# Normalised tile 3 transposed by DMA instead of by TensorE, in a gated cross-attention and mixture block on one core

## The chip, the cores and the metric

The kernel runs on one core of a Trainium2 chip. The metric is the device time of one execution, in microseconds. PE stands for TensorE (PEld for its weight loads), DVE for VectorE, ACT for ScalarE, POOL for GpSimd and SP for SyncE, which here only issues DMAs.

## The reference

The input x has 2 batches of 512 rows of 1024 floats, the context 2 batches of 1024 x 1024. What is computed, with fake_quant(v, s, z) = (clip(round(v / s + z), 0, 255) - z) * s:

```python
x = x + tanh(g_xattn) * matmul(fake_quant(layernorm(x), s1, z1), fake_quant(ctx, s2, z2))
n = layernorm(x)
gate = softmax(n @ W_gate.T)                                  # 8 experts
thr = sigmoid(n @ W_thr + b_thr) * 0.125
w = maximum(gate - thr, 0); w = w / sum(w)                    # sum 0 counts as 1
base = n @ W_base.T + b_base
moe = einsum('ner,ne,eor->no', (n @ A_w.T), w, B_w) * 2       # rank 16
x = x + tanh(g_ffn) * (base + moe)
```

## The kernel before

**Tiles.** The 1024 rows are 8 tiles t = 0 to 7 of 128 rows, tiles 0 to 3 of batch 0 and 4 to 7 of batch 1. Every engine has a hand-written order of instructions; the engines meet through semaphores, and the same names stand in each engine's list.

**Stage A, per batch, the quantised product.** `affine_q1` (ACT) and `round_q1` (DVE) turn the normalised rows into bf16 integers q1; `affine_ctx` (ACT) and `round_ctx` (DVE) do it for 8 chunks of the context. q1 of batch 0 is transposed by PE, q1 of tiles 4 to 7 by DMA (`transpose_q1` on SP, L299). `first_half` and `second_half` (L913) are the products of batch 1, `add_product` (DVE, L708) adds them to x in `xs`, POOL sums the context columns (`sum_k`, L408 and L413) for `column_sums` (L979), and adds the result (`add_columns`).

**Stage B, per tile t, the mixture.** `normalise(t)` (ACT, L511) writes the second layernorm's rows to `work`. They are needed transposed and split into a high part `lnTh` and a low part `lnTl` of type fp32r. `combined(t, i)` (PE, L1035 to L1037) multiplies them with the weights, also split, in three pieces i = 0, 1, 2 of the output columns: 24 matmuls for a piece. Piece 0 holds the gate's columns. After it come, on DVE and ACT, the steps of the gate: `gate_max` (DVE L732), `gate_exps` (ACT L542, L543), `gate_weights` (DVE L739 to L751, ends in `hw`). PE transposes `hw` in `flip_hw(t)` (L1050), ACT and DVE split that (L502, L722), and `moe` (L1059 to L1061) adds the experts' part. `add_row_term` (ACT L484), `add_bias` (POOL L430) and `finish` (DVE L763) close the tile, SP stores it.

**Two ways to transpose the normalised tile.** For tiles 0 to 4 PE does it: `flip_ln(t)` (L1023), 8 fp32 transposes of 128x128 into two PSUM banks, between `combined(t - 1, 0)` and `combined(t - 1, 1)`. ACT (`split_hi`) and DVE (`split_lo`) read the banks. The two banks 6 and 7 are used by turns by `flip_ln` and `flip_hw`, so that `flip_hw(2)` waits until DVE has read the first half of tile 3. For tiles 5 to 7 (`by_dma`) it goes by DMA: `halve(t)` (ACT L520) copies the tile as two blocks of 16-bit halves into ring slot 3, `transpose_ln(t)` (SP L292) transposes them into ring slot 4, `join(t)` (ACT L529) interleaves them to floats in ring slot 5, `joined_hi(t)` (ACT L535) and `joined_lo(t)` (DVE L726) split them.

**Order round the change.** PE does the mixture of tiles 0, 1, 2, then, at t == `A1_AFTER` = 3, both halves of batch 1's product, then the mixture of tiles 3 to 7. ACT in pass t = 1, after `split_hi(hw, 1)`: `normalise(3)`, `affine_q1(6)`, `affine_q1(7)`, `affine_ctx(11)`, `affine_ctx(12)`; in pass t = 2: `gate_exps(2)`, `add_row_term(2)`, the two `split_hi` of tile 3, `affine_ctx(13)`, `split_hi(hw, 2)`. DVE in pass t = 2: `gate_max(2)`, `gate_weights(2)`, the two `split_lo` of tile 3, `split_lo(hw, 2)`, `round_q1(7)`, `round_ctx(13)`, `finish(2)`, `round_ctx(14)`. SP: the store of tile 0, `transpose_q1` of tiles 4, 5 and 6, the store of tile 1, `transpose_q1(7)`.

**Memory.** `ring` has 6 slots of 4 KB a partition. Slots 3, 4 and 5 hold at that time the context chunks 10, 11 and 12. `colbc` (4 KB a partition) holds the regrouped weights of B until PE has transposed them in pass t = 0, and from `scale_columns(1, 0)` on the column terms of batch 1.

Of the kernel before, what the change touches and what calls it, by code (L numbers as in the profile page):

```python
# [21 lines left out]
U16 = mybir.dt.uint16  # L22
# [5 lines left out]
P = 128  # L28
# [6 lines left out]
def gated_block(nc, x, ctx_in, g_x, g_f, x1_scale, x1_zp, x2_scale, x2_zp,  # L35
                W_base, b_base, W_gate, W_thr, b_thr, A_w, B_w, out):
    B, S, D = x.shape
# [4 lines left out]
    MT = S // P  # L42
    T = B * MT
# [24 lines left out]
    turn_of = {key: n // NS + 1 for n, key in enumerate(chunks)}  # L68


    by_dma = [t for t in range(T) if t > MT]


    early = [("A", 0, 0), ("A", 0, 1), ("gates", 0, 0)] + [("W", o, i) for o in range(2) for i in range(NH)]
# [13 lines left out]
    flip_no = {key: n for n, key in enumerate(flips)}  # L88
# [32 lines left out]
    with es:  # L121
# [8 lines left out]
        ring = sb("ring", [P, NS, 2 * H])  # L130
# [38 lines left out]
        own_home["W", OWN_W + 3] = landing[:, after_WTl + 2 * O + 3 * D:after_WTl + 2 * O + 4 * D]  # L169

        halves = ring[:, 3, :].bitcast(U16)
        halvesT = ring[:, 4, :].bitcast(U16).rearrange("p (b t) -> p b t", t=P)
        lnT = ring[:, 5, :]

        def home(key):
            return own_home[key] if key in own_home else ring[:, slot_of[key], :]
# [81 lines left out]
        @block.sync  # L258
        def _(sp):
            def load_x(t):  # L260
                b, m = t // MT, t % MT
                sp.dma_start(xs[:, t, :], x[b, m * P:(m + 1) * P, :]).then_inc(x_loaded[t], 16)

            def load_own(key):
                dst, src = source(key)
                sp.dma_start(dst, src).then_inc(own_loaded[key], 16)

            def load(n):
                key = chunks[n]
                if n >= NS:  # L270
                    old = chunks[n - NS]
                    if old[0] == "ctx":
                        sp.wait_ge(ctx_affine, old[1] + 1)
                    elif old[0] == "B":
                        sp.wait_ge(b_regrouped, 1)
                    else:
                        last = (old[0], old[1], 0 if old[0] == "gates" else 1)
                        sp.wait_ge(flipped, flip_no[last] + 1)
                s = slot_of[key]
                if key[0] == "gates":  # L280
                    sp.dma_start(ring[0:E, s, :], W_gate).then_inc(slot_loaded[s], 16)
                    sp.dma_start(ring[E:E + 1, s, :], W_thr.rearrange("(a d) -> a d", a=1)).then_inc(gates_loaded, 16)
                else:
                    dst, src = source(key)
                    sp.dma_start(dst, src).then_inc(slot_loaded[s], 16)

            def transpose_ln(t):
                n = by_dma.index(t)
                sp.wait_ge(ln_halved, n + 1)
                if n:  # L290
                    sp.wait_ge(ln_joined, n)
                sp.dma_start(halvesT, halves, transpose=True).then_inc(ln_transposed[t], 16)  # L292

            def transpose_q1(t):
                m = t % MT
                sp.wait_ge(q1_ready, t + 1)
                if m == 0:
                    sp.wait_ge(prod_ready, NH * MT)
                sp.dma_start(q1T[:, :, m * P:(m + 1) * P], q1[:, t % 2, :], transpose=True).then_inc(q1_transposed[m], 16)  # L299

            for t in range(MT):
                load_x(t)
            for c in range(CPB):
                load_own(("ctx", c))
            for n in range(NS):
                load(n)
            for o in range(OWN_W, O // P):
                load_own(("W", o))
            load_x(MT)
            load_x(MT + 1)  # L310
            load(NS)
            sp.dma_start(tb[:, :], b_base.rearrange("(a d) -> a d", a=1).to_broadcast([P, O])).then_inc(s_bias, 16)
            load_x(MT + 2)
            load_x(MT + 3)
            for n in range(NS + 1, len(chunks)):
                load(n)
            for t in range(T):
                b, m = t // MT, t % MT
                if t < T - 1:
                    sp.wait_ge(out_part, NP * (t + 1))  # L320
                    sp.dma_start(out[b, m * P:(m + 1) * P, :], xs[:, t, :]).then_inc(s_stored, 16)
                    if t + 3 == A1_AFTER:
                        transpose_q1(MT)
                        transpose_q1(MT + 1)
                        transpose_q1(MT + 2)
                    if t + 2 == A1_AFTER:
                        transpose_q1(MT + 3)
                    if t + 3 in by_dma:
                        transpose_ln(t + 3)
                else:  # L330
                    for i, (_, c, n) in enumerate(outp):
                        sp.wait_ge(out_part, NP * t + i + 1)
                        sp.dma_start(out[b, m * P:(m + 1) * P, c:c + n], xs[:, t, c:c + n]).then_inc(s_stored, 16)
            sp.wait_ge(s_stored, 16 * (T - 1 + NP))
# [124 lines left out]
        def _(act):  # L459
# [12 lines left out]
            def affine_ctx(c):  # L472
                arrived(act, ("ctx", c))
                s = home(("ctx", c))
                if c >= NU:
                    act.wait_ge(q2_ready, c - NU + 1)
                nc.scalar.activation(q2u[:, c % NU, :], s, ACT.Identity, bias=Z2, scale=R2).then_inc(ctx_affine, 1)  # L477
# [36 lines left out]
            def halve(t):  # L514

                n = by_dma.index(t)
                if n:
                    act.wait_ge(ln_transposed[by_dma[n - 1]], 16)
                act.wait_ge(ln_ready, t + 1)
                nc.scalar.copy(halves.rearrange("p (h c) -> p h c", h=2),  # L520
                               work[:, t % NW, :].bitcast(U16).rearrange("p (c h) -> p h c", h=2)).then_inc(ln_halved, 1)

            def join(t):

                n = by_dma.index(t)
                if n:
                    act.wait_ge(ln_lo, n)
                act.wait_ge(ln_transposed[t], 16)
                nc.scalar.copy(lnT.bitcast(U16).rearrange("p (c h) -> p h c", h=2),  # L529
                               halvesT.rearrange("p (h k) t -> p h (k t)", h=2)).then_inc(ln_joined, 1)  # L530

            def joined_hi(t):
                act.wait_ge(ln_joined, by_dma.index(t) + 1)
                act.wait_ge(base_part, NP * (t - 1))
                nc.scalar.copy(lnTh[:, t % 2, :], lnT).then_inc(ln_hi, 1)  # L535
# [39 lines left out]
            for t in range(T):  # L575
                if t + 1 == MT:
                    normalise(MT)
                if t == 0:

                    arrived(act, ("B", 0))  # L580
                    act.wait_ge(cols_added, NH * MT - len(own_col_adds))
                    act.wait_ge(x1_part, NH * MT)
                    nc.scalar.activation(colbc[:, :].rearrange("p (j e r) -> p e j r", j=8, e=E),
                                         ring[:, slot_of["B", 0], :].rearrange("p (e j r) -> p e j r", e=E, j=8),
                                         ACT.Identity, scale=SCALING).then_inc(b_regrouped, 1)
                gate_exps(t)
                add_row_term(t)
                if t == 0:
                    for key in late[10:12]:
                        split_hi(key)  # L590
                if t + 1 in by_dma:
                    join(t + 1)
                elif t + 1 < T:
                    split_hi(("ln", t + 1, 0))
                    split_hi(("ln", t + 1, 1))
                if t + 1 == A1_AFTER:
                    affine_ctx(CPB + 5)
                split_hi(("hw", t, 0))
                if t + 1 in by_dma:
                    joined_hi(t + 1)  # L600
                if t == 0:
                    for key in late[12:]:
                        split_hi(key)
                if t + 2 < T and t + 2 != MT:
                    normalise(t + 2)
                if t + 2 in by_dma:
                    halve(t + 2)
                if t + 3 == A1_AFTER:
                    affine_ctx(CPB)
                    affine_ctx(CPB + 1)  # L610
                    affine_ctx(CPB + 2)
                    affine_q1(MT)
                    affine_q1(MT + 1)
                if t + 2 == A1_AFTER:
                    affine_q1(MT + 2)
                    affine_q1(MT + 3)
                    affine_ctx(CPB + 3)
                    affine_ctx(CPB + 4)
                if t + 1 == A1_AFTER:
                    affine_ctx(CPB + 6)  # L620
                    affine_ctx(CPB + 7)
                    scale_columns(1, 0)
                    scale_columns(1, 1)
# [546 lines left out]
```

## Time and profile before

| what | value |
|---|---|
| three runs | 185.35, 187.31 and 186.85 us, median 186.85 us |
| the profiled execution, its own time | 185.18 us |
| its span, first to last instruction | 183.4 us (1.8 us lie around it) |
| PE busy | 173.0 us |
| DVE, ACT, POOL busy | 112.8, 90.6, 71.9 us |

A busy share is a mean over stages with different limits. All times of rows are microseconds from the start of the span unless marked ns; a name like L1035 is a line of the kernel. The ends of matmuls are modelled: in a run of them their starts tell the pace.

### The profile page before, as it was taken

The numbers are of one execution on the slowest core, as the hardware profiler recorded it, in microseconds if no ns is written. First come the engines' busy times: TensorE is split into PE (matmuls) and PEld (weight loads), VectorE is DVE, ScalarE is ACT, GpSimd is POOL, SyncE is SP. The second block draws the span as 40 slices with busy tenths as digits, with TensorE's granted clock in tenths as the row PEclk, the third lists the DMA queues.
The fourth block names the chain that finished last, engine by engine and source line by source line (L and its number), as shares of the span: only waits on it lengthen the run. The fifth ranks groups of instructions, "written<-read, shape, count | busy, mean of one in ns | idle before, by whom it ended". The sixth has DMA issues, their size and how long they took to land.

```text
span 183.4 us, 2896 instructions
## 1 busy us (share of the span) xinstructions
PE 173.0 (94%) x1058; PEld 150.5 (82%) x1058; DVE 112.8 (62%) x281; ACT 90.6 (49%) x123; POOL 71.9 (39%) x89
## 2 busy tenths in 40 slices
PE   4869999989999998999899999999999999999993
PEld 4755446568899998999864479999999999999992
DVE  1999895989588988978852673583351351351331
ACT  2399914665987938194810106160970970820300
POOL 3560024921001395299868787045500500500400
PEclk9999999999999999999999999999999999999999
DMA  6999999999030332065040000006209008002003
GB/s 223 307 390 386 390 410 405 363 395 380 33 116 0 119 110 118 0 118 172 12 135 29 0 0 0 4 0 114 114 0 228 4 0 229 2 4 114 2 0 114
DMA packets 19934, 25.39 MB, mean 138 GB/s; under 512 B 11207, under 2 KB 12615, under 8 KB 19920
## 3 DMA queue, kind: packets, MB, share of 16 engines
q1 hardware_dynamic: 19906, 25.21, 40.6%
q8 instruction: 8, 0.13, 0.3%
q14 instruction: 6, 0.05, 0.1%
q10 hardware_dynamic: 14, 0.00, 0.0%
HBM read 18.39 MB, written 4.19 MB: 123 GB/s over the span
## 4 chain that ended last, share of the span: by engine, by line
PE 67%; DVE 17%; ACT 5%; DMA 4%; issue 3%; POOL 2%; DVEq 0%; ACTq 0%; POOLq 0%
PE bank L913 14%; PE bank L1035 13%; PE bank L1037 13%; PE bank L1036 13%; DVE st L654 5%; DVE q L689 2%; PE bank L995 2%; DMA q1T<-q 2%; PE bank L971 2%; DMA xs<-in_x_dram 2%; PE bank L1061 2%; PE bank L1060 2%; PE bank L1059 2%; DVE WTl L722 1%; ACT WTh L502 1%
## 5 line engine op out<-in xcount | busy, mean ns | idle before, releaser
L1035 PE MATMUL bank<-WTh,lnTh 128*128 128x388 f32 (+1 forms) x192 | 67.2, 350 | 0.0
L1037 PE MATMUL bank<-WTh,lnTl 128*128 128x388 f32 (+1 forms) x192 | 65.1, 339 | 0.0
L1036 PE MATMUL bank<-WTl,lnTh 128*128 128x388 f32 (+1 forms) x192 | 65.0, 338 | 0.0
L1035 PEld LDWEIGHTS bank<-WTh,lnTh 128*128 128x128 f32 x192 | 36.2, 189 | 0.3
L1036 PEld LDWEIGHTS bank<-WTl,lnTh 128*128 128x128 f32 x192 | 36.2, 189 | 0.0
L1037 PEld LDWEIGHTS bank<-WTh,lnTl 128*128 128x128 f32 x192 | 36.1, 188 | 0.0
L430 POOL TENSOR_TENSOR xs<-xs,tb 128x1024 f32<-128x1024 f32 x8 | 19.3, 2408 | 39.8 <-ACT xs L484 39.8
L913 PE MATMUL bank<-q,q1T 128*128 128x512 bf16 x128 | 30.3, 379 | 0.2 <-DVE q L689 0.2
L424 POOL TENSOR_TENSOR xs<-xs,colbc 128x512 f32<-128x512 f32 x14 | 18.0, 1313 | 15.9 <-DVE xs L708 11.1
L913 PEld LDWEIGHTS bank<-q,q1T 128*128 128x128 bf16 x128 | 12.1, 98 | 14.3 <-DVE q L689 0.6
L654 DVE BATCH_NORM_STATS2 st<-xs 128x6 f32<-128x512 f32 x32 | 20.7, 681 | 4.2 <-DMA xs<-in_x_dram 4.2
L763 DVE SCALAR_TENSOR_TENSOR xs<-bank,con,xs 128x250 f32<-128x250 f32 (+2 forms) x24 | 13.1, 571 | 15.4 <-PE bank L1061 11.8
L542 ACT ACTIVATE gt<-bank,con 128x1 f32<-128x1 f32 x8 | 2.1, 260 | 31.6 <-DVE gt L732 31.6
L413 POOL TENSOR_TENSOR colacc<-colacc,q 128x512 f16<-128x512 f16 x12 | 15.1, 1256 | 3.3 <-DVE q L689 2.2
L511 ACT ACTIVATE work<-xs,cf 128x1024 f32<-128x1024 f32 x8 | 10.0, 1247 | 11.0 <-POOL cf L398 11.0
L708 DVE SCALAR_TENSOR_TENSOR xs<-bank,con,xs 128x512 f32<-128x512 f32 x16 | 11.3, 745 | 6.5 <-PE bank L913 6.4
L397 POOL TENSOR_TENSOR cf<-cf,mhalf 128x1 f32<-128x1 f32 x8 | 4.4, 547 | 27.9 <-DVE cf L667 27.9
L469 ACT ACTIVATE q1u<-xs,cf 128x1024 uint8<-128x1024 f32 x8 | 9.8, 1239 | 6.6 <-DVE q L679 4.0
L502 ACT CAST WTh<-bank 128x512 fp32r<-128x512 f32 (+1 forms) x19 | 10.1, 573 | 5.8 <-PE bank L995 5.8
L689 DVE TENSOR_SCALAR q<-q2u 128x1024 bf16<-128x1024 uint8 x16 | 12.1, 777 | 0.5 <-ACT q2u L477 0.4
L722 DVE TENSOR_TENSOR WTl<-bank,WTh 128x512 fp32r<-128x512 f32 (+1 forms) x19 | 11.7, 658 | 1.1 <-ACT WTh L502 1.1
L491 ACT ACTIVATE colbc<-bank,con 128x512 f32<-128x512 f32 x4 | 2.7, 687 | 15.1 <-PE bank L979 9.5
(102 smaller groups left out, 230.7 us busy)
## 6 DMA issues: line engine op xcount, KB each, us to landing
xs<-in_x_dram SPq DMA_DIRECT2D x8, 512.0 KB, 7.3
landing<-in_ctx_dram SPq DMA_DIRECT2D x8, 512.0 KB, 10.8
ring<-in_ctx_dram SPq DMA_DIRECT2D x8, 512.0 KB, 6.8
out_dram<-xs SPq DMA_DIRECT2D x7, 512.0 KB, 2.9
ring<-in_L_ffn_W_base_dram SPq DMA_DIRECT2D x4, 512.0 KB, 13.2
landing<-in_L_ffn_W_base_dram SPq DMA_DIRECT2D x4, 512.0 KB, 15.9
ring<-in_L_ffn_A_w_dram SPq DMA_DIRECT2D x1, 512.0 KB, 12.8
ring<-in_L_ffn_B_w_dram SPq DMA_DIRECT2D x1, 512.0 KB, 6.5
```

What stands on the lines that cost most here:

```text
L413: nc.gpsimd.tensor_tensor(colacc[:, h, :], colacc[:, h, :], tile, ALU.add).then_inc(col_added, 1)
L424: nc.gpsimd.tensor_tensor(part, part, colbc[:, h * H:(h + 1) * H], ALU.add).then_inc(cols_added, 1)
L430: nc.gpsimd.tensor_tensor(xs[:, t, :], xs[:, t, :], tb[:, :], ALU.add).then_inc(xb_ready, 1)
L502: nc.scalar.copy(hi, src).then_inc(flip_hi, 1)
L654: nc.vector.bn_stats(st[:, t, h, :], xs[:, t, h * H:(h + 1) * H]).then_inc(dve_step, 1)
L689: nc.vector.tensor_scalar(q, q2u[:, c % NU, :].rearrange("p (k n) -> p k n", k=2), -CENTRE, None, ALU.add).then_inc(q2_ready, 1)
L722: nc.vector.tensor_tensor(lo, src, hi.bitcast(F32), ALU.subtract).then_inc(flip_read, 1)
L763: nc.vector.scalar_tensor_tensor(out=part, in0=bank[3 * j + i][:, a:a + n], scalar=TGF, in1=part, op0=ALU.mult, op1=ALU.add).then_inc(out_ ...
L913: return mm(bank[prod_bank(h, m)][:, :], q1T[:, k, m * P:(m + 1) * P], q2[:, k, h * H:(h + 1) * H], start=(k == 0), stop=(k == KT - 1))
L1035: mm(o, hi, WTh[:, k, a:b], start=(k == 0), stop=False, skip_group_check=True)
L1036: mm(o, hi, WTl[:, k, a:b], start=False, stop=False, skip_group_check=True)
L1037: ins = mm(o, lo, WTh[:, k, a:b], start=False, stop=(k == KT - 1), skip_group_check=True)
```

## The change

Tile 3 joins the tiles that are transposed by DMA. PE's `flip_ln(3)`, ACT's two `split_hi` and DVE's two `split_lo` of tile 3 are gone. ACT does `halve(3)` after `normalise(3)`, `join(3)` at the end of pass t = 1 and `joined_hi(3)` in pass t = 2 after `add_row_term(2)`; DVE does `joined_lo(3)` after `split_lo(hw, 2)`. SP issues `transpose_ln(3)` between `transpose_q1(5)` and `transpose_q1(6)`. Since chunks 11 and 12 still hold slots 4 and 5 then, tile 3's transposed halves go to `colbc`, and the joined tile of every `by_dma` tile now goes to slot 3, over the halves. So `halve` of a later tile waits for `joined_lo` of the tile before it, where it waited for its transpose.

```diff
-    by_dma = [t for t in range(T) if t > MT]
+    by_dma = [MT - 1] + [t for t in range(T) if t > MT]
...
-        halvesT = ring[:, 4, :].bitcast(U16).rearrange("p (b t) -> p b t", t=P)
-        lnT = ring[:, 5, :]
+        lnT = ring[:, 3, :]
+
+        def halvesT(t):
+
+            return (colbc[:, :] if t < MT else ring[:, 4, :]).bitcast(U16).rearrange("p (b t) -> p b t", t=P)
...
                 if n:
                     sp.wait_ge(ln_joined, n)
-                sp.dma_start(halvesT, halves, transpose=True).then_inc(ln_transposed[t], 16)
+                else:
+                    sp.wait_ge(flipped, flip_no["B", 0, 1] + 1)
+                sp.dma_start(halvesT(t), halves, transpose=True).then_inc(ln_transposed[t], 16)
...
                         transpose_q1(MT + 1)
+                        transpose_ln(MT - 1)
                         transpose_q1(MT + 2)
                     if t + 2 == A1_AFTER:
                         transpose_q1(MT + 3)
-                    if t + 3 in by_dma:
+                    if t + 3 in by_dma and t + 3 > MT:
                         transpose_ln(t + 3)
...
                 if n:
-                    act.wait_ge(ln_transposed[by_dma[n - 1]], 16)
+                    act.wait_ge(ln_lo, n)
                 act.wait_ge(ln_ready, t + 1)
...
             def join(t):
 
-                n = by_dma.index(t)
-                if n:
-                    act.wait_ge(ln_lo, n)
                 act.wait_ge(ln_transposed[t], 16)
...
-                if t + 1 in by_dma:
+                if t + 1 in by_dma and t + 1 > MT:
                     join(t + 1)
+                elif t + 1 in by_dma:
+                    joined_hi(t + 1)
                 elif t + 1 < T:
                     split_hi(("ln", t + 1, 0))
                     split_hi(("ln", t + 1, 1))
                 if t + 1 == A1_AFTER:
                     affine_ctx(CPB + 5)
                 split_hi(("hw", t, 0))
-                if t + 1 in by_dma:
+                if t + 1 in by_dma and t + 1 > MT:
                     joined_hi(t + 1)
...
                     affine_ctx(CPB + 3)
                     affine_ctx(CPB + 4)
+                    join(MT - 1)
```

## Rows read from the trace of the kernel before

**Rows 1.** The page: busy time by engine, and TensorE's granted clock in 40 slices.
```profile
PE 173.0 (94%) x1058; PEld 150.5 (82%) x1058; DVE 112.8 (62%) x281; ACT 90.6 (49%) x123; POOL 71.9 (39%) x89
...
PEclk9999999999999999999999999999999999999999
```

**Rows 2.** Timelines of PE and PEld: start us, us, instruction, idle before, releaser.
```profile
86.77 0.34 PE L1037 MATMUL bank<-WTh,lnTl 128*128 128x388 f32 x1
87.83 0.30 PE L1050 MATMUL bank<-idf,hw 128*128 128x128 f32 x1 [0.72 <-DVE lnTl L722]
...
93.63 1.90 PE L913 MATMUL bank<-q,q1T 128*128 128x512 bf16 x8
...
100.72 0.10 PEld L979 LDWEIGHTS bank<-colacc,ones_h 128*128 128x128 f16 x1 [0.29 <-issue]
```

**Rows 3.** Chain that ended last: start us, us, what.
```profile
77.49 3.67 DMA q1T<-q
...
87.01 0.68 DVE lnTl L722
...
88.13 0.18 PE bank L1035
...
112.30 0.87 PE bank L1023 x8
```

**Rows 4.** Timeline of ACT, passes t = 1 and t = 2.
```profile
72.26 1.25 ACT L511 ACTIVATE work<-xs,cf 128x1024 f32<-128x1024 f32 x1
77.50 2.38 ACT L469 ACTIVATE q1u<-xs,cf 128x1024 uint8<-128x1024 f32 x2 [3.99 <-DVE q L679]
79.79 2.36 ACT L477 ACTIVATE q2u<-ring,prm,con 128x1024 uint8<-128x1024 f32 x2
84.94 0.26 ACT L542 ACTIVATE gt<-bank,con 128x1 f32<-128x1 f32 x1 [2.79 <-DVE gt L732]
```

**Rows 5.** Timeline of DVE, pass t = 2.
```profile
86.66 0.35 DVE L751 SCALAR_TENSOR_TENSOR hw<-bank,gt 128x128 f32<-128x128 f32 x1
...
88.98 1.21 DVE L679 TENSOR_SCALAR_CACHE_REDUCE q<-q1u 128x1024 bf16<-128x1024 uint8 x1
```

**Rows 6.** Timeline of SP's queue: issue us, us, instruction.
```profile
77.49 2.69 SPq L299 DMA_TRANSPOSE q1T<-q  x2
...
82.52 1.23 SPq L299 DMA_TRANSPOSE q1T<-q  x1
...
90.22 1.24 SPq L299 DMA_TRANSPOSE q1T<-q  x1
```

**Rows 7.** q1 transposes (L299): from issue to landing, four of them.
```profile
DMA to landing us min/median/max: 3.0/3.1/3.7
```

**Rows 8.** Transposes of halves (L292), tiles 5 to 7: issue duration, landing.
```profile
L292 SPq DMA_TRANSPOSE ring<-ring x3: 1774/1849/1992, 124.0 to 150.5; - x3
...
DMA to landing us min/median/max: 4.2/4.3/6.0
```

**Rows 9.** Lines of tiles 5 to 7: duration ns min/median/max, first and last start.
```profile
L520 ACT COPY ring<-work x3: 1900/1900/1902, 122.1 to 148.5; 128x2048 uint16<-128x2048 uint16 x3
...
L529 ACT COPY ring<-ring x3: 2547/2547/2547, 129.6 to 157.7; 128x2048 uint16<-128x2048 uint16 x3
...
L535 ACT CAST lnTh<-ring x3: 1050/1051/1051, 132.2 to 160.5; 128x1024 fp32r<-128x1024 f32 x3
...
L726 DVE TENSOR_TENSOR lnTl<-ring,lnTh x3: 1224/1226/1226, 133.3 to 161.6; 128x1024 fp32r<-128x1024 f32 x3
```

**Rows 10.** ACT behind a join, pass t = 4.
```profile
129.64 2.55 ACT L529 COPY ring<-ring 128x2048 uint16<-128x2048 uint16 x1
132.03 0.28 ACT L502 CAST hwTh<-bank 128x128 fp32r<-128x128 f32 x1
```

**Rows 11.** Timeline of POOL: column additions that end before TensorE's 100.72.
```profile
91.13 2.41 POOL L413 TENSOR_TENSOR colacc<-colacc,q 128x512 f16<-128x512 f16 x2 [0.63 <-DVE q L689]
95.13 5.48 POOL L413 TENSOR_TENSOR colacc<-colacc,q 128x512 f16<-128x512 f16 x4 [1.59 <-DVE q L689]
```

More of the change, by code:

```diff
@@ L523, in join @@
             def join(t):
-                n = by_dma.index(t)
-                if n:
-                    act.wait_ge(ln_lo, n)
                 act.wait_ge(ln_transposed[t], 16)
                 nc.scalar.copy(lnT.bitcast(U16).rearrange("p (c h) -> p h c", h=2),
-                               halvesT.rearrange("p (h k) t -> p h (k t)", h=2)).then_inc(ln_joined, 1)
+                               halvesT(t).rearrange("p (h k) t -> p h (k t)", h=2)).then_inc(ln_joined, 1)
             def joined_hi(t):
```

## The prediction

> **What bounds the kernel now.** I read the page first [rows 1]: PE is busy 173.0 of 183.4 us, the next engine 112.8, and the granted clock is full (1.00, its 2.4 GHz level) in every slice. So time is saved where PE has less to do or waits less, and lost where it is made to wait. The reader should then ask at which places PE waits. Around the change there is one, in PE's timeline [rows 2]: the last matmul of `combined(2, 1)` starts at 86.77, and at the pitch of 0.18 of such matmuls [rows 3] PE would be free at 86.95; `flip_hw(2)` starts at 87.83. 0.88 us are lost. From there PE runs through `combined(2, 2)` and `moe` to the first product of batch 1 at 93.63 [rows 2], 5.80 us without a wait, and from then on to the end nothing but PE's own work is of weight in the chain.
>
> What does `flip_hw(2)` wait for? The row names DVE's `lnTl`, and the chain says the same: DVE reads the first half of tile 3 from the bank for 0.68 us from 87.01, and 0.14 later PE starts [rows 2, 3]. But `hw` itself is only ready at 86.66 + 0.35 = 87.01 [rows 5]. Two conditions lie 0.68 us apart. Further back stands `gate_exps(2)` on ACT at 84.94, which had waited 2.79 us for DVE's `gate_max` [rows 4]; DVE was late with it since it was rounding q1 and ctx, behind a q1 transpose of 3.67 us [rows 3]. From `gate_exps(2)` to `hw` ready is 87.01 - 84.94 = 2.07 us, a chain of small steps with no room.
>
> **What is taken away.** PE loses the 8 transposes of tile 3. In the chain the same 8 of tile 4 stand for 0.87 us [rows 3]. By that PE comes to `flip_hw(2)` at 86.95 - 0.87 = 86.08. It can't start there: `hw` is ready at 87.01. The bank wait goes too, as no tile 3 halves pass through the banks. So if nothing else moved, `flip_hw(2)` would start at 87.01 + 0.14 = 87.15, against 87.83: 0.68 us gained. The 0.87 of the transposes is hidden behind the gate and is not added. ACT's two splits and DVE's two are replaced by one of 1.05 on ACT and one of 1.23 on DVE [rows 9], about equal work.
>
> **What is added on ACT, and where it lands.** `halve(3)` takes 1.90 us [rows 9]. It follows `normalise(3)`, from 72.26 to 73.5, and ACT's next work starts at 77.50 after an idle 3.99 us [rows 4]: hidden, with 2 us to spare, cost nothing. `join(3)` takes 2.55 us [rows 9] and is queued between `affine_ctx(12)`, which ends at 79.79 + 2.36 = 82.15, and `gate_exps(2)`, now at 84.94 [rows 4]. The gap is 2.79 us, just long enough, if the join could start at 82.15 to 82.4. The question is whether tile 3's transpose has landed by then.
>
> It hasn't. SP issues q1's transposes of tiles 4 and 5 from 77.49 for 2.69 us, to 80.18, since they wait for DVE's `round_q1` [rows 6], and `transpose_ln(3)` stands behind them in SP's queue. Its own conditions (halves ready at 75.4, `colbc` free) are long met, so it is issued at 80.2. The three transposes of the same kind took 4.2, 4.3 and 6.0 us from issue to landing [rows 8]. Bounds: 84.4 with the shortest, 86.2 with the longest. Neighbours in the queue matter: of q1's four transposes [rows 7], the shortest had 3.0 and one 3.7, and the 3.7 is the one with another transpose right behind it [rows 3, 6]. Tile 3 has q1's tile 6 behind it, issued at 82.52 [rows 6]; SP is free for that by 80.2 + 1.8 = 82.0 [rows 8], so q1 itself isn't late. I take 4.3 plus 0.4, somewhat over half of q1's 0.7, landed at 84.9.
>
> The join then runs from 84.9; behind a join of 2.55 us the next instruction started 2.4 us after the join's start in one pass [rows 10], so I take 2.5 between that and the full length. `gate_exps(2)` starts at 87.45 in place of 84.94: 2.5 later. `hw` is ready 2.07 later, at 89.52, and `flip_hw(2)` starts at 89.66. Against 87.83 that is **+1.83 us**. Queued behind ACT's wait stand `gate_exps(2)`, `add_row_term(2)` and all of pass t = 2; PE, DVE and POOL wait for them. PE, free at 86.08, stands still for 3.6 us.
>
> The Trainium skill speaks against this change: "VectorE: DVE Perf Modes", Rules for kernel authors, says to transpose 128x128 on TensorE if a PSUM destination is fine, and by DMA otherwise. By it the sum would be a loss, and the working above agrees. A tile of halves is 512 KB, twice one of q1, and its shortest landing is 1.2 us longer, 4.2 against 3.0 [rows 7, 8]: 2.4 us for the 512 KB. "Advanced Engine Details and Errata", X-Bar Transpose, in the Trainium skill, expects 350 to 400 GB/s, by which they would take, as an estimate, 1.4 us; the landing would be 1.0 earlier and the loss 1.1 in place of 2.1. The rows decide.
>
> **The second place, tile 7 of q1.** In pass t = 2 all of ACT's list moves by 2.5. DVE's `round_q1(7)` was at 88.98 [rows 5] and stood behind `split_lo(hw, 2)`; now `joined_lo(3)`, 1.23 us [rows 9], stands between them, where the two splits it replaces stood before both and filled a wait of DVE. So `round_q1(7)` starts at 88.98 + 2.5 + 1.2 = 92.7, the transpose of tile 7 is issued at 90.22 + 3.7 = 93.9 [rows 6] and has landed at 96.9 to 97.0 [rows 7]. PE's product starts at 89.66 + 5.80 = 95.46 and comes to tile 7 after six of the eight matmuls that the row has in 1.90 us [rows 2], 1.3 us: 96.8. Before, it had landed at 93.2 and was wanted at 94.9, 1.7 us of cover; now the cover is gone and PE waits about 0.3 with the semaphore's delay. Bounds 0 and 0.7, the last if the landing takes 3.7. POOL meets it at the same point: its column additions of chunk 13 wait for `round_ctx(13)` and move 3.7, from 91.13 to 94.85, end at 97.3, and push those of chunks 14 and 15 (5.48 us from 95.13, end 100.61, PE's `column_sums(1)` at 100.72) by 2.1 in all [rows 2, 11]. That is the same 1.83 + 0.3, side by side, counted once.
>
> **Later tiles.** `halve(6)` and `halve(7)` now wait for `joined_lo` of the tile before. That takes 1.23 on DVE after `joined_hi`, while ACT does `normalise` in about 1.25 [rows 4, 9]: 0.1 later on ACT at most, and the transpose's wait is off PE's path. Nothing, for both.
>
> **The sum.** 1.83 + 0.3 = +2.1 us. Against the profiled execution, 185.18 (183.4 of span and 1.8 around it), that is 187.3. The median of the runs is 186.85, 1.67 above that execution; the same difference on it gives **188.9**, which I forecast, 1.1% slower. Within the mechanism: the join at 84.4, followed 2.4 later, and tile 7 in time gives +1.1; at 85.1 with the full 2.55 and 0.7 for tile 7 gives +2.8.
>
> **Rivals.**
> - *The join fits the gap* (other side: faster). If the transpose landed by 82.4, `gate_exps(2)` would stay at 84.94 and 0.68 us would be gained: 186.2. The point from which it decides is a landing at 84.9 - 1.83 = 83.1, 2.9 us after the issue. For it: ACT's gap is 2.79 us. Against: the shortest of three needs 4.2 [rows 8]. Chance 0.07.
> - *About even.* The landing comes a little sooner than any row (a faster transfer, as above), or the steps of the gate are quicker when DVE has nothing else to do: -0.4 to +1.1, 186.5 to 187.9. Chance 0.14.
> - *A slow transpose.* One of three took 6.0 [rows 8]. Landed at 86.2, everything is 1.3 later: +3.4, 190.3. Chance 0.12 for the median of several runs.
> - *The clock falls.* PE stands still for 3.6 us, while in the rows the clock is full throughout and there is no standstill of PE that long behind the start. At the lower level the 0.18 of a matmul becomes 0.36; the 5.80 us up to the product would take up to 11.6, of which I take a third, +1.9: +4, 190.9. Chance 0.05. The Trainium skill, "TensorE: Matmul & The Clock Gate", Part 1, states that an idle TensorE is set back to half clock; no row here shows it.
> - The forecast, +1.1 to +2.8 (187.9 to 189.7), has the other 0.62.
>
> **How the numbers follow.** About 1% (1.87 us) is what a measurement of this kernel can tell from no change; three runs spread over 1.96. Of the forecast's 0.62 some 0.34 lies above that bound, with 0.17 of the slow rivals 0.51: slower. Same: 0.28 of the forecast, 0.14, and most of the first rival, 0.46. Faster 0.03. The range leaves out the clock's case and the faster half of the first: 186.1 to 190.4.
>
> **What the profile will show.** ACT: L520 with about 1.9 us near 73.5, in idle time; L529 for tile 3 starting at 84.4 to 85.1, its releaser a DMA to `colbc`, and L542 right behind it near 87.4, no longer waiting for DVE. PE: 8 fewer L1023; L1050 of tile 2 after an idle of over 3 us, released by DVE's `hw`, not `lnTl`. SP: a third transpose at 80.2. PE idle of some tenths before the eighth product of batch 1. It would be wrong if the landing were under 3 us after the issue, or if PE had later waits that take the delay in; I found none.

## The result, and the profile after

The changed kernel takes 190.19 us (median of 6 runs, 189.26 to 190.38), the kernel before 186.66 (6 runs, 185.35 to 187.95). The ratio is 1.0186, 95% interval 1.0147 to 1.0225: 3.5 us slower. The profiled execution took 189.26 us with a span of 187.5, against 185.18 and 183.4. Beside the experiments the kernel before was measured again, 17 to 29 runs, medians 186.35 to 186.40; one execution of e3_ln_first that took 957.16 us is left out of its ratio.

Near the start the executions differ for reasons that have nothing to do with the change: in 8 of the 14 traces the clock falls once there, in the fourth slice of the page, and in others the work is late without that (`flip_hw(1)` starts at 72.70 in e1_late_join and at 73.18 in e9_warm_late_lo). So traces are compared below by their distance from `flip_hw(1)`, which starts at 71.73 before and at 71.94 after. 0.2 us of every difference between the two traces is that.

The page of the changed kernel, its busy times and its granted clock:

```profile
PE 173.2 (92%) x1044; PEld 151.2 (81%) x1050; DVE 113.3 (60%) x280; ACT 94.9 (51%) x124; POOL 71.9 (38%) x89
...
PEclk9999999999999999999699999999999999999998
```

PE has the same busy time with 8 transposes less (PEld counts them, 1058 to 1050; some records of matmuls are missing), and the clock, which was full everywhere [rows 1], has a slice of 0.6. Both are signs of matmuls that went slower. SP's queue comes first in time (issue us, us), then the time from issue to landing of the transposes of halves:

```profile
77.70 2.70 SPq L304 DMA_TRANSPOSE q1T<-q  x2
80.50 1.92 SPq L297 DMA_TRANSPOSE colbc<-ring  x1
82.73 1.50 SPq L304 DMA_TRANSPOSE q1T<-q  x1
...
95.44 1.25 SPq L304 DMA_TRANSPOSE q1T<-q  x1
```
```profile
L297 SPq DMA_TRANSPOSE colbc<-ring x1: 1918/1918/1918, 80.5 to 80.5; - x1
...
DMA to landing us min/median/max: 4.2/4.3/5.2
```

Tile 3's transpose is issued at 80.50, right behind q1's two and as they end, as forecast. It is the one that took 5.2 us, so it landed at 85.7. ACT's timeline:

```profile
73.75 1.90 ACT L526 COPY ring<-work 128x2048 uint16<-128x2048 uint16 x1
...
85.73 2.48 ACT L532 COPY ring<-colbc 128x2048 uint16<-128x2048 uint16 x1 [3.38 <-DMA colbc<-ring]
88.09 0.24 ACT L545 ACTIVATE gt<-bank,con 128x1 f32<-128x1 f32 x1
...
91.59 0.25 ACT L508 CAST hwTh<-bank 128x128 fp32r<-128x128 f32 x1
```

`halve(3)` (73.75) lies in idle time. `join(3)` starts at 85.73, after an idle 3.38 us that the DMA ended, and `gate_exps(2)` is queued behind it: 88.09 in place of 84.94 [rows 4], 2.94 later with the traces aligned. PE and PEld:

```profile
86.08 0.34 PE L1043 MATMUL bank<-WTh,lnTl 128*128 128x388 f32 x1
90.20 0.33 PE L1056 MATMUL bank<-idf,hw 128*128 128x128 f32 x1 [3.78 <-DVE hw L757]
...
91.11 0.53 PE L1041 MATMUL bank<-WTh,lnTh 128*128 128x386 f32 x1
91.44 0.52 PE L1042 MATMUL bank<-WTl,lnTh 128*128 128x386 f32 x1
...
94.40 0.34 PE L1043 MATMUL bank<-WTh,lnTl 128*128 128x386 f32 x1
```
```profile
97.58 1.41 PEld L919 LDWEIGHTS bank<-q,q1T 128*128 128x128 bf16 x8 [0.17 <-issue]
...
104.72 0.10 PEld L985 LDWEIGHTS bank<-colacc,ones_h 128*128 128x128 f16 x1 [0.33 <-issue]
```

PE was free at 86.26, 0.90 us earlier with the traces aligned, and then stood still until 90.20, 3.78 us by its row, released by `hw`. Before it was 87.83 and released by `lnTl` [rows 2]: 2.2 later aligned. Then look at the distance between starts: 0.33 from 91.11 to 91.44, where it is 0.18 at the full clock. The stretch up to the first product of batch 1 took 97.58 - 90.20 = 7.38 us, before 5.80 [rows 2]: 1.58 more. Windows of 2 us show the clock (us, PE busy and its count, clock, DMA share, GB/s):

```profile
88.00:90.00 2.00, 0.00 (x0) 1.00 0.00 0
90.00:92.00 2.00, 1.80 (x7) 0.66 0.00 0
92.00:94.00 2.00, 2.00 (x7) 0.50 0.00 0
94.00:96.00 2.00, 2.00 (x14) 0.99 0.00 0
```

No work at all, then half the clock (1.2 GHz) from some tenths after PE's start at 90.20, then the full one again. From the first product on the traces run 3.7 to 3.9 us apart up to the end. Last, DVE and POOL in pass t = 2:

```profile
92.08 2.19 DVE L732 TENSOR_TENSOR lnTl<-ring,lnTh 128x1024 fp32r<-128x1024 f32 x1
94.20 1.21 DVE L685 TENSOR_SCALAR_CACHE_REDUCE q<-q1u 128x1024 bf16<-128x1024 uint8 x1
```
```profile
92.03 1.17 POOL L414 TENSOR_TENSOR colacc<-q 128x512 f16<-128x512 bf16 x1
```

`joined_lo(3)` took 2.19 us. The same instruction takes 1.23 for tiles 5 to 7 [rows 9]. Beside it stands an addition on POOL. Behind it `round_q1(7)` starts at 94.20 and the transpose of tile 7 is issued at 95.44, the last row of SP's queue above.

### The profile page after: what moved, and what is told of

The parts are those of the page before. It is cut to its first block, busy times and chain, and to the rows that moved or that the text cites. A ratio compares the mean times of both kernels' runs of the same rounds, so it can differ in the third digit from the quotient of the medians.

```text
span 187.5 us, 2874 instructions
## 1 busy us (share of the span) xinstructions
PE 173.2 (92%) x1044; PEld 151.2 (81%) x1050; DVE 113.3 (60%) x280; ACT 94.9 (51%) x124; POOL 71.9 (38%) x89
## 4 chain that ended last, share of the span: by engine, by line
PE 66%; DVE 16%; ACT 5%; DMA 5%; issue 4%; POOL 2%; SPq 1%; DVEq 0%; ACTq 0%; POOLq 0%
PE bank L919 14%; PE bank L1041 13%; PE bank L1043 13%; PE bank L1042 13%; DVE st L660 5%; DMA colbc<-ring 3%; PE bank L1001 2%; PE bank L977 2%; DMA xs<-in_x_dram 2%; PE bank L1067 2%; PE bank L1066 2%; PE bank L1065 2%; DVE WTl L728 1%; ACT WTh L508 1%; PE bank L1029 1%
## 5 line engine op out<-in xcount | busy, mean ns | idle before, releaser
L1043 PE MATMUL bank<-WTh,lnTl 128*128 128x388 f32 (+1 forms) x192 | 65.8, 343 | 0.0
L1041 PEld LDWEIGHTS bank<-WTh,lnTh 128*128 128x128 f32 x192 | 36.8, 192 | 0.3
L1042 PEld LDWEIGHTS bank<-WTl,lnTh 128*128 128x128 f32 x192 | 36.7, 191 | 0.0
L1043 PEld LDWEIGHTS bank<-WTh,lnTl 128*128 128x128 f32 x192 | 36.6, 191 | 0.0
L919 PE MATMUL bank<-q,q1T 128*128 128x512 bf16 x122 | 29.1, 379 | 0.8 <-DVE q L695 0.5
```

The costliest lines, as they stand in the source:

```text
L919: return mm(bank[prod_bank(h, m)][:, :], q1T[:, k, m * P:(m + 1) * P], q2[:, k, h * H:(h + 1) * H], start=(k == 0), stop=(k == KT - 1))
L1041: mm(o, hi, WTh[:, k, a:b], start=(k == 0), stop=False, skip_group_check=True)
L1042: mm(o, hi, WTl[:, k, a:b], start=False, stop=False, skip_group_check=True)
L1043: ins = mm(o, lo, WTh[:, k, a:b], start=False, stop=(k == KT - 1), skip_group_check=True)
```

## The experiments

The places by which they are compared, worked out from PEld's timelines (us from `flip_hw(1)`; the product is batch 1's first, column sums are `column_sums(1)`; the ratio is to the kernel before, from the timed runs):

```
kernel              flip_hw(2)  product  column sums  end     ratio (95% interval)
before                16.07      21.90      28.99    111.67
changed               18.26      25.64      32.78    115.56   1.0186 (1.0147, 1.0225)
e1_late_join          15.40      21.23      29.19    112.00   1.0021 (1.0002, 1.0040)
e2_warm               18.39      24.22      32.91    115.62   1.0200 (1.0177, 1.0224)
e3_ln_first           15.63      21.46      29.47    112.22   1.0030 (1.0010, 1.0049)
e4_none               15.34      21.18      28.28    111.12   0.9969 (0.9955, 0.9983)
e5_slots              16.09      21.92      29.01    111.68   1.0012 (0.9988, 1.0035)
e6_late_both          15.35      21.18      28.28    111.10   0.9959 (0.9940, 0.9979)
e7_q1_first           18.36      25.70      32.80    115.76   1.0199 (1.0166, 1.0233)
e8_q1_first_warm      18.30      24.13      31.83    114.74   1.0170 (1.0143, 1.0197)
d4_delay              17.51      24.87      31.97    114.65   1.0143 (1.0097, 1.0189)
d5_delay              18.60      27.02      34.12    116.80   1.0226 (1.0185, 1.0266)
e9_warm_late_lo       18.27      24.10      31.21    114.02   1.0140 (1.0096, 1.0183)
e10_gate_first        14.15      20.10      28.11    110.83   0.9968 (0.9943, 0.9993)
```

The theory is called A in all of them: the gate's steps are queued behind `join(3)` on ACT, PE stands still for them, and the clock falls in the standstill or soon after it.

**e1_late_join.** The join where ACT has time.

```diff
 # ACT, end of pass t = 1
-                    join(MT - 1)
 # ACT, pass t = 2
-                elif t + 1 in by_dma:
-                    joined_hi(t + 1)
...
                     affine_ctx(CPB + 7)
+                    join(MT - 1)
+                    joined_hi(MT - 1)
 # DVE, behind split_lo(hw, t)
-                if t + 1 in by_dma:
+                if t + 1 in by_dma and t + 1 > MT:
                     joined_lo(t + 1)
 # DVE, behind round_ctx(CPB + 7)
+                    joined_lo(MT - 1)
                     add_product(1, 0, 0)
```

> The changed kernel with join(3) and joined_hi(3) moved behind affine_ctx(15) on ACT and joined_lo(3) behind round_ctx(15) on DVE. Theory A (the loss is the gate's steps queued behind join(3) on ACT, and the clock that falls in the standstill): flip_hw(2) starts about 0.7 us before its place in the kernel before, released by DVE's hw, the clock stays at 1.00, and the time is 0.7 us under the kernel before, 4.2 under the changed one. Theory B (the loss comes from the third transpose's traffic, or from the shared slot and the new waits of the later tiles): those are all still here, so the time stays 2 to 4 us above the kernel before.

`flip_hw(2)` starts at 15.40, 0.67 us before its old place, and the clock is full there. That is A, and the third transpose, the shared slot and the new waits are all still here. But the end is 0.33 later than before, not 0.7 earlier. DVE, POOL and PE tell why:

```profile
96.06 2.18 DVE L731 TENSOR_TENSOR lnTl<-ring,lnTh 128x1024 fp32r<-128x1024 f32 x1
```
```profile
95.43 6.35 POOL L419 TENSOR_TENSOR colacc<-colacc,q 128x512 f16<-128x512 f16 x4 [0.88 <-DVE q L694]
```
```profile
101.92 0.38 PE L985 MATMUL bank<-colacc,ones_h 128*128 128x512 f16 x1 [0.69 <-POOL colacc L419]
```

`joined_lo(3)` took 2.18 us here too, beside POOL's column additions, which took 6.35 in place of 5.48 [rows 11], 0.87 longer, and PE waited 0.69 for them. The two hold each other up. The Trainium skill states this in "SBUF — State Buffer", SBUF: two separate sides: a DVE operation with two SBUF inputs and a GpSimd operation that reads SBUF use one pair of ports in turn, each for its whole length. The 2.18 and 6.35 agree with it, and so do e3_ln_first, e7_q1_first and e10_gate_first below.

**e2_warm.** The standstill filled with small matmuls.

```diff
 # PE, flip_hw(t)
+                if t == 2:
+                    pe.wait_ge(out_part, NP * 2)
+                    for _ in range(62):
+                        mm(bank[3][:, 0:P], idb[:, :], idb[:, :], start=True, stop=True)
                 pe.wait_ge(hw_ready, t + 1)
```

> The changed kernel with 62 small matmuls (128x128 bf16, into bank 3, which is free then) in front of the wait for hw in flip_hw(2); they end before hw is ready. Theory A with the clock as a cost of its own: flip_hw(2) stays where it is, about 2.2 us behind the kernel before, the granted clock stays 1.00 and the stretch from flip_hw(2) to the first product of batch 1 takes 5.8 us in place of 7.6: the time is 1.8 us under the changed kernel and about 2.1 above the kernel before. Rival: the slow matmuls come from traffic or from another engine, or the wait for tile 7 of q1 takes the place of the clock (0.3 us): the gain is under 0.5, or 1.5.

The clock stayed full, and the stretch from `flip_hw(2)` to the product took 5.83 us. The slow matmuls were the standstill's. Yet the rival was right too, with more than its 0.3 us: the time is as long as the changed kernel's, and at the column sums the two are 0.13 apart.

```profile
87.31 3.64 PE L1057 MATMUL bank<-idb 128*128 128x128 bf16 x62
91.37 0.33 PE L1060 MATMUL bank<-idf,hw 128*128 128x128 f32 x1 [0.43 <-DVE hw L757]
...
99.73 0.61 PE L919 MATMUL bank<-q,q1T 128*128 128x512 bf16 x2 [1.06 <-DMA q1T<-q]
...
105.92 0.38 PE L985 MATMUL bank<-colacc,ones_h 128*128 128x512 f16 x1 [0.19 <-POOL colacc L419]
```

PE waits 1.06 for the DMA of tile 7 of q1 and 0.19 for POOL. The product came 1.4 us sooner and wasn't allowed to go on. So the fall of the clock and the late tile 7 lie side by side, and the first hid the second. POOL's four additions took 5.48 here: they are late, behind DVE's list, and not slow.

**e3_ln_first.** The transpose ahead of q1's in SP's queue.

```diff
+                        transpose_ln(MT - 1)
                         transpose_q1(MT)
                         transpose_q1(MT + 1)
-                        transpose_ln(MT - 1)
```

> The changed kernel with transpose_ln(3) ahead of transpose_q1(4) in SP's queue, everything else as changed. Theory A, with the landing as the cause: issued at 75.7, landed at about 80, so join(3) starts at 82.2 when ACT is free, gate_exps(2) stands near 84.9 to 85.3, flip_hw(2) near 87.2 to 87.6 and the clock is full: 0.2 to 0.7 us under the kernel before. q1's transpose of tile 4 lands up to 0.5 later, and DVE's round_q1(6) behind it. Rival (the join itself is too long for ACT wherever the transpose lands): 1 us or more above the kernel before.

ACT and PE:

```profile
83.41 2.54 ACT L532 COPY ring<-colbc 128x2048 uint16<-128x2048 uint16 x1
86.58 0.26 ACT L545 ACTIVATE gt<-bank,con 128x1 f32<-128x1 f32 x1 [0.63 <-DVE gt L738]
```
```profile
88.72 0.33 PE L1056 MATMUL bank<-idf,hw 128*128 128x128 f32 x1 [1.15 <-DVE hw L757]
...
96.37 0.60 PE L919 MATMUL bank<-q,q1T 128*128 128x512 bf16 x2 [0.35 <-POOL colacc L419]
```

The join starts as ACT comes free, and `gate_exps(2)` waits for DVE again, 0.29 later than before, since DVE's `round_q1(6)` ahead of `gate_max(2)` waits for the later q1 transposes. `flip_hw(2)` is 0.44 earlier than before, so the landing was the cause of the late gate, and the rival falls. At the end it is 0.55 later than before: `joined_lo(3)` is still ahead of `round_q1(7)`, PE stands before tile 7's product (the row calls POOL; PEld waits for the transpose there) and again for POOL's column additions. The second place shows here without a long standstill before it. DVE and POOL held each other up here as well, `joined_lo(3)` with 1.51 us and POOL's addition with 2.17 in place of 1.18:

```profile
90.60 1.51 DVE L732 TENSOR_TENSOR lnTl<-ring,lnTh 128x1024 fp32r<-128x1024 f32 x1
```
```profile
90.97 2.17 POOL L414 TENSOR_TENSOR colacc<-q 128x512 f16<-128x512 bf16 x1
```

**e4_none.** Tile 3's transposes and splits left out (its mixture is computed from what tile 1 left behind).

```diff
 # PE, DVE and ACT, the same condition in all; the two waits for these transposes go as well
-                if t + 1 < T and t + 1 not in by_dma:
+                if t + 1 < T and t + 1 not in by_dma and t != 2:
```

> The kernel before with PE's 8 transposes of tile 3 and the four splits left out and nothing in their place (tile 3's mixture is computed from what tile 1 left in lnTh and lnTl). Theory A: the upper bound of what the change can give, 0.7 us (0.68 at flip_hw(2), as hw is ready at 87.01), not the 0.87 of the transposes alone, nor more. Rival: PE's work counts in full or DVE's and ACT's splits were in the way as well: 0.9 to 2 us.

0.55 us less in the trace, 0.9969 in the runs, 0.6 us. `flip_hw(2)` is 0.73 earlier and is released by `hw`:

```profile
88.23 0.33 PE L1050 MATMUL bank<-idf,hw 128*128 128x128 f32 x1 [0.86 <-DVE hw L751]
```

So the gain to be had here was 0.6 to 0.7, and the 0.87 of the transposes doesn't count in full.

**e5_slots.** The shared slot alone, in the kernel before.

```diff
-        lnT = ring[:, 5, :]
+        lnT = ring[:, 3, :]
 # halve(t)
-                    act.wait_ge(ln_transposed[by_dma[n - 1]], 16)
+                    act.wait_ge(ln_lo, n)
 # join(t)
-                n = by_dma.index(t)
-                if n:
-                    act.wait_ge(ln_lo, n)
```

> The kernel before, with tile 3 still on TensorE, and only the shared slot taken over: the joined tile of tiles 5 to 7 goes to slot 3 over the halves, and halve(6) and halve(7) wait for joined_lo of the tile before. Theory A: ACT's halves start about 0.1 us later, which the wait for the transpose hides: no difference, within 0.3 us. Theory B (the shared slot is part of the loss): 0.5 us or more above the kernel before.

1.0012, and every place is within 0.02 us of the kernel before. The slot and the waits of the later tiles cost nothing.

**e6_late_both.** e1 with `joined_lo(3)` later.

```diff
 # against e1_late_join, DVE
                     round_ctx(CPB + 7)
-                    joined_lo(MT - 1)
                     add_product(1, 0, 0)
                     add_product(1, 0, 1)
                     add_product(1, 0, 2)
                     add_product(1, 0, 3)
+                    joined_lo(MT - 1)
```

> As e1_late_join, but joined_lo(3) behind the first four add_product of batch 1 on DVE, where POOL has nothing to do until ACT has scaled the columns. Theory C (from e1_late_join: joined_lo and POOL's column additions hold each other up, 2.18 us in place of 1.23 and 6.35 in place of 5.48, and TensorE's column_sums(1) waits for POOL): joined_lo(3) takes under 1.9 us, POOL's last four additions 5.5, column_sums(1) doesn't wait for them, and the time is 0.9 us under e1_late_join, 0.6 to 0.7 under the kernel before. Rival (e1's loss is something else, the join's traffic or ACT): as e1_late_join, 0.3 above the kernel before.

0.9959 (0.9940 to 0.9979): 0.8 us under the kernel before (0.57 in the traces), 1.2 under e1_late_join, as theory C has it. POOL's last four additions take 5.48 again and the wait at the column sums is gone. `joined_lo(3)` took 2.05, not under 1.9, since POOL had begun with `add_columns`, but nobody on PE's path waits for that:

```profile
102.47 2.05 DVE L731 TENSOR_TENSOR lnTl<-ring,lnTh 128x1024 fp32r<-128x1024 f32 x1
```
```profile
95.28 5.48 POOL L419 TENSOR_TENSOR colacc<-colacc,q 128x512 f16<-128x512 f16 x4 [0.89 <-DVE q L694]
```
```profile
87.95 0.33 PE L1056 MATMUL bank<-idf,hw 128*128 128x128 f32 x1 [0.87 <-DVE hw L756]
...
100.92 0.38 PE L985 MATMUL bank<-colacc,ones_h 128*128 128x512 f16 x1
```

**e7_q1_first and e8_q1_first_warm.** `round_q1(7)` ahead of `joined_lo(3)`, without and with the small matmuls of e2.

```diff
 # DVE, pass t = 2, both kernels; the 62 matmuls of e2_warm in e8 alone
-                if t + 1 in by_dma:
+                if t + 1 in by_dma and t + 1 > MT:
                     joined_lo(t + 1)
...
                     round_q1(MT + 3)
+                    joined_lo(MT - 1)
```

> The changed kernel with round_q1(7) ahead of joined_lo(3) on DVE. If the clock and the wait for tile 7 lie side by side: flip_hw(2) and the slow matmuls stay as they are, tile 7 was covered by them anyway, and the time stays within 0.4 us of the changed kernel. If the wait for tile 7 is the one that decides even there: 1 us or more less.

> e7_q1_first and e2_warm together: 62 small matmuls ahead of the wait in flip_hw(2), and round_q1(7) ahead of joined_lo(3). If each of the two was hidden behind the other, only both together give something: the clock stays full, tile 7 has landed in time, and the time is 1.5 us under the changed kernel, 2.3 above the kernel before, which is the lateness of flip_hw(2) alone. Rival (the 3.9 us have one more cause that neither touches): above 3.5.

e7: nothing gained, 1.0199. e8: tile 7 is in time, the product and its first column sums run on, but at `column_sums(1)` PE waits for POOL, and the end is 0.82 us under the changed kernel, not 1.5. `column_sums(1)` stands 2.84 us after its place in the kernel before, 0.6 more than the 2.2 of `flip_hw(2)`:

```profile
104.62 0.38 PE L986 MATMUL bank<-colacc,ones_h 128*128 128x512 f16 x1 [0.43 <-POOL colacc L419]
```

In e7 `joined_lo(3)` had no POOL beside it, and took what it takes for the other tiles:

```profile
94.32 1.22 DVE L732 TENSOR_TENSOR lnTl<-ring,lnTh 128x1024 fp32r<-128x1024 f32 x1
```

**e9_warm_late_lo.** The changed kernel with e2's matmuls and with `joined_lo(3)` at e6's place; the join stays ahead of the gate.

```diff
 # against e2_warm, DVE
-                if t + 1 in by_dma:
+                if t + 1 in by_dma and t + 1 > MT:
                     joined_lo(t + 1)
...
                     add_product(1, 0, 3)
+                    joined_lo(MT - 1)
```

> The changed kernel with the 62 small matmuls of e2_warm and with joined_lo(3) where e6_late_both has it, so that DVE's and POOL's work behind the gate is as in the kernel before; join(3) stays ahead of gate_exps(2). What is left is the lateness of flip_hw(2) alone: 2.2 us above the kernel before at flip_hw(2), at the first product and at the end. Rival (e8_q1_first_warm's 0.6 us more at column_sums(1) have another cause than DVE's round_ctx(14) and joined_lo): 2.8.

`flip_hw(2)`, the product and the column sums are all 2.20 to 2.22 later than before, the end 2.35. With e2 (behind the gate, the late tile 7 without the fall of the clock), e7 (the fall, with tile 7 in time) and this one (neither), the parts are told apart: 2.2 for the late gate, and 1.6 behind it, which either of the two gives (the late tile 7 together with POOL's late additions).

**d4_delay and d5_delay.** The kernel before with nothing but a delay on ACT.

```diff
 # ACT, end of pass t = 1, 4 or 5 times
+                    for i in range(4):
+                        nc.scalar.copy(colbc[:, :], colbc[:, :]).then_inc(act_step, 1)
+                        act.wait_ge(act_step, i + 1)
```

> The kernel before, tile 3 on TensorE, with four copies of colbc onto itself (values that nobody needs) at the place of join(3) on ACT, some 5.2 us from 82.2: no third transpose, no shared slot. Theory A: gate_exps(2) starts 2.4 us later, flip_hw(2) 1.7 later, TensorE stands still for about 2.6 us, the clock stays full: 1.7 us above the kernel before. If the clock falls after so short a standstill: 3.3 above.

> As d4_delay with five copies, some 6.5 us. Theory A: gate_exps(2) 3.7 us later, flip_hw(2) 3.0 later, a standstill of about 3.9 us as in the changed kernel, the granted clock falls to 0.5 behind it as there, and the stretch up to the first product takes about 7.4 us in place of 5.8: 4.6 us above the kernel before. If the fall of the clock belongs to the transposes or to the dropped matmuls of tile 3, not to the standstill: 3.0 above.

The copies took 1.07 us each, not 1.3, so `flip_hw(2)` was 1.44 and 2.53 later, not 1.7 and 3.0. In both the clock fell, and in d4 I had not expected it. PE of d4, and its clock:

```profile
87.99 0.34 PE L1040 MATMUL bank<-WTh,lnTl 128*128 128x388 f32 x1
90.49 0.30 PE L1053 MATMUL bank<-idf,hw 128*128 128x128 f32 x1 [2.16 <-DVE lnTl L725]
```
```profile
90.00:92.00 2.00, 1.51 (x9) 0.96 0.00 0
92.00:94.00 2.00, 2.00 (x8) 0.50 0.00 0
94.00:96.00 2.00, 2.00 (x10) 0.68 0.69 131
```

PE stood still for 2.3 us (2.16 by the row, with the modelled end of the last matmul), ran on at the full clock for more than a microsecond, and then at half. Against the kernel before, the stretch up to the product took 1.5 us more in d4 (7.36) and 2.6 in d5 (8.42). In d5 the clock fell while PE still stood, and was down from 89.5 to 96.3:

```profile
89.50:90.00 0.50, 0.00 (x0) 0.50 0.00 0
```

The ends are 3.0 and 5.1 us later in the traces, 2.7 and 4.2 by the ratios; expected were 3.3 with a fall of the clock, and 4.6. No transpose by DMA and no dropped matmul is needed for it: a late gate in this kernel does it.

**e10_gate_first.** e6 with the last wait for `hw` taken away as well.

```diff
 # against e6_late_both, DVE, pass t = 1
                     round_ctx(CPB + 3)
-                    round_ctx(CPB + 4)
 # DVE, pass t = 2
                 gate_weights(t)
+                if t + 1 == A1_AFTER:
+                    round_ctx(CPB + 4)
```

> As e6_late_both, with round_ctx(12) on DVE moved from before gate_max(2) to behind gate_weights(2). In e6_late_both TensorE still waits 0.9 us for hw at flip_hw(2), since gate_max(2) is queued behind two round_ctx. Theory A: gate_max(2) starts 1.0 us or more earlier, flip_hw(2) no longer waits, 0.8 us under e6_late_both, 1.4 to 1.5 under the kernel before. Rival (POOL's column additions or the steps up to moe take over): the same as e6_late_both.

```profile
87.10 0.27 PE L1057 MATMUL bank<-idf,hw 128*128 128x128 f32 x1
...
100.91 0.38 PE L986 MATMUL bank<-colacc,ones_h 128*128 128x512 f16 x1 [0.74 <-POOL colacc L419]
```

`flip_hw(2)` no longer waits and is 1.20 earlier than in e6, but at the column sums only 0.17 are left: PE waits 0.74 for POOL's additions. 0.9968, the same as e6 within the intervals. The rival was right: behind the gate POOL is next. `joined_lo(3)`, with the same place in the list as in e6, began before POOL's `add_columns` and took 1.22 us here.

## Why the prediction was right, point by point

It forecast slower, 188.9 (186.1 to 190.4), +2.1 us; measured were 190.19 and +3.5. The direction, the place and the mechanism of the gate were right, and the size was 1.4 us short. Against the later medians of the kernel before (186.35 to 186.40) the same 190.19 is +3.8, and the traces have +3.9, so the shortfall is rather 1.7 or 1.8. The 190.19 lies inside the range that was given but above 189.7, the end of the forecast's own mechanism: that it fell under 190.4 is luck, for that bound was drawn for a slow transpose, with the case of the clock left out. The ends of that mechanism, added up again, are +1.2 and +2.7, not +1.1 and +2.8.

- *PE's 0.87 is hidden behind the gate; 0.68 to be had.* Right: 0.73 in e4 at `flip_hw(2)`, 0.6 in the time.
- *`halve(3)` costs nothing; the later tiles cost nothing.* Right: 73.75 in idle time, and e5 at 1.0012.
- *The landing at 84.9.* It was 85.7, 85.5 aligned: 5.2 us from issue to landing, within the bounds of 4.2 and 6.0. Instead of 4.3 and 0.4 for its neighbour it was 4.3 and 0.9.
- *`flip_hw(2)` 1.83 later.* 2.2 (e9 shows this part alone, at all places).
- *0.3 for tile 7 of q1.* **This is the term that was mis-sized.** It is 1.1 us of waiting at tile 7 and 1.6 to 1.7 in all behind the gate with POOL's additions (e2 against e9: 1.70 at the column sums). I had put `joined_lo(3)` at 1.23 us from tiles 5 to 7, where POOL is idle; beside POOL's addition it took 2.19. POOL's additions were in the rows, and I read them for their own lateness alone. With 1.0 us from this and 0.4 from the gate, tile 7's transpose was issued 1.3 later than forecast, 95.2 aligned in place of 93.9.
- *The clock falls, chance 0.05.* It fell, in the profiled run (mean clock 0.988). Three of the other runs have 0.980 to 0.982, where no run of the kernel before is under 0.988: they had this fall and the one near the start. For the last two, 0.988 and 0.991, the mean doesn't tell which fall it was. The price, +1.9, was near its 1.58, and the chance far off. The time stayed under this rival's 190.9 for a reason that I had not seen: the fall and the late tile 7 don't add up, as e2 and e7 show.
- *The join fits the gap* was the rival on the other side. It needed a landing under 2.9 us after the issue; e3 shows that with an early landing the gate is in time.

## What to carry to other kernels

Before work is put on an engine that has idle time, look at what is queued behind it there and when its input lands. The join fitted ACT's idle 2.79 us by its length and stood ahead of the gate that PE needs; behind `affine_ctx(15)` and with `joined_lo(3)` out of POOL's way it costs nothing, and the same change is then 0.8 us faster than the kernel before. Where a large change has one effect, take it away alone before it is called the cause: here either of two was enough for the last 1.6 us.

## What the runs showed of the hardware

- TensorE's granted clock fell to half in or after standstills, by their rows, of 2.16 us (d4_delay), 3.27 (d5_delay) and 3.78 (the changed kernel), and not after those of 0.86 to 1.15 us of e1, e3, e4 and e6. It fell while PE stood only in d5. In the changed kernel PE had run at the full clock for 0.4 us again, in e7_q1_first and d4 for 1.3. The fall cost 1.5, 2.6 and 1.6 us. That an idle TensorE is set back to half clock is the rule of the Trainium skill, "TensorE: Matmul & The Clock Gate", Part 1, that the prediction named; the runs agree in that each fall goes with a standstill, and differ in that most of them came when PE was at work again.
- Small matmuls on a free bank kept it full through the same gap (e2_warm, e8, e9).
- A DVE subtraction of two 128x1024 float tensors in SBUF took 1.22 to 1.23 us alone, 2.05 to 2.21 when it began beside a POOL addition, and 1.51 when it began towards the end of one (e3_ln_first); POOL's four additions took 6.35 in place of 5.48.
- A DMA transpose of 512 KB took 4.2 to 4.4 us from issue to landing in most cases, 5.8 to 6.0 for tile 6 in the kernel before [rows 8], d4, d5 and e5, 4.9 to 5.1 once in each of e2, e8 and e9, and 5.2 to 5.3 as the longest in each of the kernels that had q1's transposes right ahead of tile 3's and behind it. No run tells why.
